# Ten row buffers and six weight buffers for the routed blocks, and two setup steps moved to GpSimd

## The reference

```python
scores = sigmoid(xf @ gate_w + bias)
top_scores, top_idx = top_k(scores, 2)                # 2 of 8 experts for each token
hact = gelu(einsum('th,ehi->tei', xf, up_w) + up_b)   # width 128 -> 512
eo   = einsum('tei,eih->teh', hact, down_w) + down_b  # 512 -> 128
out  = shared + einsum('teh,te->th', eo * 0.1, w)     # w: the tokens' weights
out  = out / (max|out| + 1e-6)
```

## Time and profile before

| | |
|---|---|
| median of 3 runs | 1534.47 us (1529.25 to 1539.84) |
| the profiled execution's own time | 1538.37 us |
| its span | 1536.6 us |
| PE busy | 1331.8 us, 87% of the span |
| DVE, ACT, POOL busy | 63%, 53%, 35% |
| transfers | 125.86 MB, 82 GB/s over the span |
| first stretch of blocks | 763.85 to 873.80 us |
| second stretch of blocks | 1362.28 to 1472.22 us |
| setup, first instruction to barrier | 0 to about 27 us |

### The profile page before, as it was taken

One profiled execution on the slowest core, in us unless ns is written; L12 is line 12 of the kernel. 1 busy time (PEld: TensorE's weight loads), 2 busy tenths in 40 slices (PEclk: granted clock), 3 DMA queues, 4 the chain that ended last, 5 costly groups with the idle time before them and its releaser, 6 DMA issues. The chain is left out here.

```text
span 1536.6 us, 27757 instructions
## 1 busy us (share of the span) xinstructions
PE 1331.8 (87%) x8392; PEld 718.9 (47%) x8392; DVE 963.3 (63%) x2050; ACT 820.1 (53%) x1727; POOL 543.9 (35%) x741
## 2 busy tenths in 40 slices
PE   2896899999999789699977896898998879987797
PEld 1671222222222268477777663221222257777665
DVE  5687788988889367441222275799999942232237
ACT  0220788888888624344345453665765444444542
POOL 3122233231231032353033303788887715113310
PEclk9995899999999989799999997799989889999999
DMA  5820222122221020112145311444444321145522
GB/s 108 123 84 1 69 79 73 33 75 80 73 73 33 2 34 2 49 35 60 51 126 145 116 44 56 141 161 145 145 139 146 99 64 51 29 106 140 142 79 69
DMA packets 133378, 125.86 MB, mean 82 GB/s; under 512 B 30764, under 2 KB 98298, under 8 KB 133257
## 3 DMA queue, kind: packets, MB, share of 16 engines
q1 hardware_dynamic: 126592, 115.63, 27.3%
q0 software_dynamic: 4544, 8.47, 1.6%
q10 hardware_dynamic: 2120, 0.28, 0.2%
HBM read 90.35 MB, written 31.34 MB: 79 GB/s over the span
## 5 line engine op out<-in xcount | busy, mean ns | idle before, releaser
L1193 DVE TENSOR_REDUCE at_nm<-at_mx 128x2 f32<-128x1024 f32 x256 | 304.0, 1220 | 40.8 <-PE at_mx L1036 39.4
L1139 ACT ACTIVATE at_probs<-at_ring 128x512 f32<-128x512 f32 x512 | 269.4, 605 | 47.5 <-PE at_ring L1048 45.8
L1553 ACT ACTIVATE m_hidden<-m_pU,m_up_b 128x512 f32<-128x512 f32 x192 | 131.1, 687 | 118.5 <-PE m_pU L1796 116.8
L1803 PEld LDWEIGHTS m_pD<-m_down,m_hidden 128*128 128x128 f32 x1536 | 177.4, 192 | 17.7 <-issue 17.7
L2345 POOL TENSOR_TENSOR ss_hc<-ss_h,ss_c_all 128x512 f32<-128x512 f32 x128 | 161.6, 1269 | 53.9 <-DVE ss_h L2515 47.6
L1803 PE MATMUL m_pD<-m_down,m_hidden 128*128 128x128 f32 x1536 | 177.6, 275 | 0.0
L1796 PE MATMUL m_pU<-m_xT_all,m_up 128*128 128x512 f32 x384 | 175.4, 603 | 2.5 <-DVE m_yt L1777 1.4
L1048 PE MATMUL at_ring<-at_qq,at_kk 51*128 51x512 bf16 x512 | 163.4, 386 | 7.0 <-ACT at_probs L1139 6.1
L1036 PE MATMUL at_mx<-at_kk,at_qq 48*128 48x512 bf16 x512 | 155.8, 397 | 13.7 <-DVE at_nm L1193 9.1
L2515 DVE TENSOR_TENSOR_SCAN ss_h<-ss_pA,ss_beta 128x512 f32<-128x512 f32 x128 | 155.2, 1215 | 15.1 <-issue 6.5
L1524 POOL DMA_INDIRECT pair_rows<-m_y,m_y_id x78 | 75.7, 970 | 238.7 <-DVE m_y L1781 227.5
(11 more groups left out here) (341 smaller groups left out, 2036.7 us busy)
## 6 DMA issues: line engine op xcount, KB each, us to landing
ss_dtb<-ss_dt_rows SPq DMA_DIRECT2D x128, 256.0 KB
m_up_now<-in_L_ffn_up_w_dram SPq DMA_DIRECT2D x78, 256.0 KB
at_qq<-q_stack SPq DMA_DIRECT2D x64, 96.0 KB, 2.3
at_kk<-k_stack SPq DMA_DIRECT2D x64, 96.0 KB, 2.3
sorted_rows<-empty_row SPq DMA_DIRECT2D x2, 2535.0 KB, 24.4
m_xb<-sorted_rows SPq DMA_DIRECT2D x78, 65.0 KB
m_down_all<-in_L_ffn_down_w_dram SPq DMA_DIRECT2D x16, 256.0 KB, 4.5
m_up_now<-pair_rows SPq DMA_DIRECT2D x16, 256.0 KB, 3.2
```

Source lines behind the costliest of these rows:

```text
L1139: act.activation(probs[:, (slot % 2) * GH + ORDER[j], :], ring[bank][:, :], ACT.Exp, scale=SCALE).then_inc(s.exp_done, 1)
L1193: dve.tensor_reduce(nm[group % 2][:, 2 * (pair % 2) + parity, 2 * half:2 * half + 2], mx[parity][:, :, :], AX.X, ALU.max, negate=True).the ...
L1553: act.activation(hidden[t % 2][:, k, :], pU[k][:, :], ACT.Gelu, bias=up_b[buf][:, k:k + 1]).then_inc(s.gelu_done, 1)
L1803: last = pe.matmul(pD[t % 2][:, c, :], hidden[t % 2][:, k, c * P:(c + 1) * P], down[buf][:, k, :], start=(k == 0), stop=(k == NI - 1))
```

## The change

- Rows: ten buffers in place of four. The first four stay in the tile `xb`, the other six lie in `hidden[1]`, three in each of its parts 0 and 3. SP issues the load of block j when DVE has finished block j-10.
- Up weights: six buffers in place of four; the two new ones are parts 1 and 2 of `hidden[1]`.
- Two waits guard the shared tile: SP, before the load of block 4, waits until the last dense down product ahead of the blocks is done; ACT, before the Gelus of the second sequence of the first dense expert behind the blocks, waits until DVE has finished all blocks.
- Setup: the four instructions that split `bd1` and the addition into `sel` are issued by POOL instead of DVE.

```diff
@@ adapter_weights, gpsimd
+        pool.wait_ge(ld2, 128)
+        pool.wait_ge(mk, 6)
+        pool.tensor_copy(w.bd1_parts[:, :], bd1[:, :]).then_inc(bp, 1)
+        pool.wait_ge(bp, 1)
+        pool.tensor_tensor(bd1_rest[:, :], bd1[0:64, :], w.bd1_parts[0:64, :], ALU.subtract).then_inc(bp, 1)
+        pool.wait_ge(bp, 2)
+        pool.tensor_copy(w.bd1_parts[0:64, :], bd1_rest[:, :]).then_inc(bp, 1)
+        pool.wait_ge(bp, 3)
+        pool.tensor_tensor(w.bd1_parts[0:32, :], bd1_rest[0:32, :], w.bd1_parts[0:32, :], ALU.subtract)
+        pool.tensor_tensor(w.sel[R0:R0 + 1, :, R0:R0 + D], w.sel[R0:R0 + 1, :, R0:R0 + D],
+                          base_at[R0:R0 + 1, :].rearrange("p (a o) -> p a o", a=1).broadcast_to([1, E0, D]), ALU.add)
@@ adapter_weights, vector: the same five instructions are gone
...
-X_BUFS, Y_BUFS, T_BUFS, U_BUFS = 4, 6, 3, 4
+OWN = 4
+X_BUFS, Y_BUFS, T_BUFS, U_BUFS = 10, 6, 3, 6
@@ moe_ffn
-        xb = sb("xb", [P, X_BUFS, ROW])
+        own_x = sb("xb", [P, OWN, ROW])
+        xb = [own_x[:, i, :] for i in range(OWN)]
+        xb += [hidden[1][:, k, i * ROW:(i + 1) * ROW] for k in (0, 3) for i in range(L // ROW)]
...
-        up_now = [sb(f"up_now{i}", [P, I1]) for i in range(U_BUFS)]
+        up_now = [sb(f"up_now{i}", [P, I1])[:, :] for i in range(OWN)] + [hidden[1][:, k, :] for k in (1, 2)]
@@ sync
             for j in range(HB):
+                if j == OWN:
+                    sp.wait_ge(s.down_done, ND * 2 * trips + NB)
                 load_block(j)
                 load_up(j)
@@ scalar, expert(n, buf, place, trip, last)
                 for t in range(ND):
+                    if last == 0 and t == 1:
+                        act.wait_ge(s.y_ready, HB)
                     gelus(n, buf, t)
```

More of the change, by code:

```diff
@@ L268, in _ @@
         dve.wait_ge(mk, 6)
[L270 to L279, removed]
         dve.wait_ge(tr, 1)
@@ L1398, in moe_ffn @@
         out_b = [sb(f"out_b{i}", [P, NC, D]) for i in range(2)]
-        xb = sb("xb", [P, X_BUFS, ROW])
-        passed = xb[0:1, :, :].rearrange("p i r -> p (i r)")[:, 0:HB * E1].rearrange("p (j e) -> p j e", j=HB)
+        own_x = sb("xb", [P, OWN, ROW])
+        passed = own_x[0:1, :, :].rearrange("p i r -> p (i r)")[:, 0:HB * E1].rearrange("p (j e) -> p j e", j=HB)
+        xb = [own_x[:, i, :] for i in range(OWN)]
+        xb += [hidden[1][:, k, i * ROW:(i + 1) * ROW] for k in (0, 3) for i in range(L // ROW)]
         hid = [hidden[0][:, i, :].rearrange("p (k t) -> p k t", k=NI) for i in range(T_BUFS)]
         xT = [hidden[0][:, T_BUFS, i * P:(i + 1) * P] for i in range(T_BUFS)]
-        up_now = [sb(f"up_now{i}", [P, I1]) for i in range(U_BUFS)]
+        up_now = [sb(f"up_now{i}", [P, I1])[:, :] for i in range(OWN)] + [hidden[1][:, k, :] for k in (1, 2)]
         order = [up_now[r // 2][:, (r % 2) * DT * E1:(r % 2 + 1) * DT * E1].rearrange("p (t e) -> p t e", t=DT)
@@ L1408, in moe_ffn @@
         y_id = [sb(f"y_id{i}", [P, 1], mybir.dt.int32) for i in range(Y_BUFS)]
-        yb = [[up_now[2 * i + k][:, :].rearrange("p (c d) -> p c d", c=NC) for k in range(2)] for i in range(2)]
+        yb = [[up_now[2 * i + k].rearrange("p (c d) -> p c d", c=NC) for k in range(2)] for i in range(2)]
         pU = [ps(f"pU{i}", [P, L]) for i in range(NI)]
@@ L1441, in load_block @@
                     sp.wait_ge(s.y_ready, j - X_BUFS + 1)
-                sp.dma_start(xb[:, j % X_BUFS, :], sorted_rows[j * P:(j + 1) * P, :]).then_inc(xb_in[j % X_BUFS], 16)
+                sp.dma_start(xb[j % X_BUFS], sorted_rows[j * P:(j + 1) * P, :]).then_inc(xb_in[j % X_BUFS], 16)
             def load_up(j):
@@ L1447, in load_up @@
                     sp.wait_ge(s.bup_done, j - U_BUFS + 1)
-                sp.dma_start(up_now[j % U_BUFS][:, :], ins["L1_ffn_up_w"][e]).then_inc(up_in[j % U_BUFS], 16)
+                sp.dma_start(up_now[j % U_BUFS], ins["L1_ffn_up_w"][e]).then_inc(up_in[j % U_BUFS], 16)
             def load_results(b):
@@ L1774, in blocks @@
                     dve.wait_ge(xb_in[j % X_BUFS], 16 * (j // X_BUFS + 1))
-                    dve.tensor_copy(y_id[j % Y_BUFS][:, :], xb[:, j % X_BUFS, ID:ID + 1])
+                    dve.tensor_copy(y_id[j % Y_BUFS][:, :], xb[j % X_BUFS][:, ID:ID + 1])
                     dve.wait_ge(s.bdown_done, j + 1)
@@ L1780, in blocks @@
                     dve.wait_ge(s.y_taken, j + 1)
-                    dve.tensor_scalar(y[j % Y_BUFS][:, :], yt[j % 2][:, :], xb[:, j % X_BUFS, WEIGHT:ROW], None, ALU.mult
+                    dve.tensor_scalar(y[j % Y_BUFS][:, :], yt[j % 2][:, :], xb[j % X_BUFS][:, WEIGHT:ROW], None, ALU.mult
                                       ).then_inc(s.y_ready, 1)
@@ L1843, in turn @@
                     pe.wait_ge(s.xT_taken, j - 1)
-                pe.transpose(pU[2 + j % 2][:, 0:P], xb[:, j % X_BUFS, 0:D], g.identf[:, :]).then_inc(s.turned, 1)
+                pe.transpose(pU[2 + j % 2][:, 0:P], xb[j % X_BUFS][:, 0:D], g.identf[:, :]).then_inc(s.turned, 1)
             def block_up(j):
```

## The result

| | before | after |
|---|---|---|
| median of the runs on one chip | 1533.38 us (4 runs) | 1468.21 us (4 runs, 1464.85 to 1468.73) |
| ratio, 95% interval | | 0.9583 [0.9552, 0.9613] |
| profiled execution, its own time | 1538.37 us | 1468.73 us |
| first stretch of blocks | 109.95 us | 77.02 us |
| second stretch of blocks | 109.94 us | 77.12 us |

The change makes the kernel 65 us faster in the medians. The two profiled executions are 69.6 us apart, since that of before lies above its median. Of these, 2.4 us have been gained when the first stretch begins (761.47 in place of 763.85), 32.9 and 32.8 us are the two stretches, 1.6 us lie between them, and behind the second one nothing changed.

What follows compares the result with a forecast made beforehand. PE was taken to be bound in the blocks by late row loads; 25.0 us from each of two stretches plus 1.8 from the setup, 51.8 us off the median of 1534.5, gave 1483 us, range 1472 to 1498.

Steps and rivals of the forecast that it cites:

- What bounds the kernel: In the block stretches PE was paced by waits for late row loads, 23.0 us a stretch, all to go.
- How long a round is without the wait: Blocks: a round without waits was put at 2.12 us, midway between 2.175 and 2.07, giving 78.4 us for 37 rounds.
- Six weight buffers: Blocks: give nothing alone, but let SP run on past the weights, held at six rounds instead of four.
- The new waits of SP and ACT: SP's wait before block 4 and ACT's behind the blocks cost 0, unless DVE fell some 3 us behind PE.
- What is late next: Blocks: PE binds narrowly; ACT's chain leaves 0.6 us a round, POOL's puts at 1.89 us leave 0.2 us.
- The setup: Five instructions moved from DVE to POOL let the copy PE waits for, and all behind it, come 1.8 us earlier.
- Rival 1: Setup and blocks: DVE and POOL hinder each other, costing the setup's 1.8 us and 5 us in blocks; 1490; chance 0.18.
- Rival 2: Blocks: transfers become the bound, rounds of say 2.5 us, a gain of 11 us per stretch, time 1511; chance 0.13.
- Rivals 3 and 4: Blocks: loads slow with number in flight, only setup gains, 1533, chance 0.04; puts' waits pace blocks, 1548, chance 0.03.

## Why the prediction was wrong in the size, point by point

- **What bounds the kernel: right.** PE waited for rows' loads, and all of these waits went. In the words on record, "All 23.0 us go"; the changed kernel's list has no load in it. The loads run ahead, by a little less than the "10 us or more" of the forecast: that of block 20 is issued at 1352.41, and PE turns that block at 1362.06; in this stretch the lead is 7 to 10 us from block 4 on, and it is enough. The lower granted clock in a piece of the first stretch went with the waits, as said: 1.00 in both stretches.
- **How long a round is without the wait: this step failed.** It said "I take the middle, 2.12 us" between a mean of 2.175 and one round of 2.07. The rounds take 1.90. Both inputs still had a wait in them. The mean was net of the printed idle, which leaves out the 0.34 us that a wait adds around itself; the one round read "without a wait" stood directly behind one, and such rounds last about 2.06 us also with five buffers, where the others last 1.90. 37 x (2.12 - 1.90) = 8 us in each stretch, 16 us in both, is more than the 13 us that the forecast lacks in the medians. Against the profiled execution: 52 + 16 = 68 of 69.6 us. In the set with eleven runs of before the gain is 59 us and the forecast lacks only 7. That it comes so near there is luck: the waits were read in an execution with stretches of 110 us, where that of the setup alone has 102 with the same four buffers, so a part of the waits that is not typical was counted as gain, and it made up for a part of what the too long round took from it. The remark that a matmul followed by a wait is "drawn to its full length" had the right mechanism and was then used for a middle, not for a lower bound.
- **The right price stood in the trace of before.** The chain of waits of the kernel before, in the dense experts:

```profile
1284.24 3.57 PE m_pD L1803 x32
```

  That is 0.112 us a matmul. The forecast used this pace itself, in what it says on ACT: "about 1.0 us for its transpose and up products" is nine matmuls, and 17 of them are 1.9 us. A round has 1 + 8 + 8 = 17 of them: 1.90 us. That times 37, and 6.45 us for the end, is 76.7 us for a stretch, against 77.0 and 77.1 measured.
- **Six weight buffers: right, and less than was said for them.** "This alone gives nothing" holds; that it "matters because it lets SP run on past the weights" doesn't: four give the same time, with ten row buffers and with six.
- **The new waits of SP and ACT: right**, cost 0. The four lines of PE's waits hold neither, in either stretch.
- **What is late next: half right.** PE binds. ACT covers its work in the shorter round too. The reading that POOL "leaves 0.2 us" took PE's pace for POOL's: puts can start 1.28 us apart.
- **The setup: right.** 1.8 us were said, and the last copy starts 1.94 us earlier. POOL started its part at about 15.5 us and not at 17.2, since its loads had landed by then.
- **Rival 1, DVE and POOL:** the hindrance happened and was free. DVE's L285 took 1.98 us under POOL's addition of 2.17 us, and L292 started only behind it, at 20.37; PE's products, which L292 needs too, ended at 20.32. So the copy L636 still came the full 1.94 us earlier. POOL had begun its long addition before L283, and was done with it at 20.07, not at 22.3. Had POOL ended at 22.3, L285 would have kept L292 waiting for about as long as the setup had gained. In the blocks puts stayed at 0.97 us.
- **Rival 2, the transfers:** 180 GB/s and a share of 0.63 to 0.65 with no wait for a load. Refuted.
- **Rivals 3 and 4:** the rounds fell from 2.80 to 1.90 us, and neither puts nor DVE appear in PE's waits within the stretch. Refuted.
- **The range** reached down to a round of 2.07 and a few us below. Its lower end had to come from the matmuls' own spacing, 1.90 us: 2 x 33.2 + 1.8 = 68.2 us, 1466.

## What to carry to other kernels

Price a loop that will no longer wait by its instructions at the pace that they have in a dense stretch of the same trace, not by the old period less the printed idle. An engine's pace read in a loop that another one sets is the other's pace. Before a gain that was read in one execution is taken off a median, look at how much its waits vary between executions. A buffer count is worked out in rounds: each further row buffer gave a load one more round of 1.9 us before PE asked for it, and four, five and six buffers give 1528, 1483 and 1467 us, while ten give nothing more.

## What was not expected of the hardware

- A wait of PE costs about 0.3 us beside its printed idle: a mean of 2.175 us of net round with late loads, 2.20 and 2.24 with a wait for ACT in each round, against 1.90 without.
- The length of a stretch that is bound by late loads varies between executions, from 101.7 to 110.1 us over those with four row buffers, while the changed kernel's is 77.0 or 77.1 in all four stretches of its two profiles.
- With half of the down products, several engines pause together for 2 us or so, three times in the two stretches, and don't when the puts are left out. The cause stays open.
- Two instructions of DVE ended 0.08 us behind the memset of POOL that ran beside them, and one in the setup 0.08 us behind POOL's addition; a copy from PSUM beside the same addition lost nothing.
- Behind 3.64 us of idle PE, with a mean granted clock of 0.57, eight matmuls lasted 1.93 us in place of 1.16, so an idle time ahead of a burst was paid for a second time.
